# Conditioning by channel-tile pairs of one condition, with the second condition of a batch placed behind the first of the next

## The chip, the cores and the metric

One core of a Trainium2 chip runs one program. The metric is the device time of one execution in microseconds. The engines are TensorE (PE), VectorE (DVE), ScalarE (ACT), GpSimd (POOL) and SyncE (SP, which only issues DMAs); each takes its own instructions in order and waits on semaphores for the others.

## The reference

There are B = 4 batches of T = 512 tokens with C = 512 channels. `x` is conditioned twice, a gated recurrence stands between, and a mixture of experts follows. In short:

```python
def bi_wkv(r, k, w, u, t):            # v = k = fside
    tf = sigmoid(sum(t))
    decay = exp(-exp(w)) * (0.5 + 0.5 * tf)
    ek = exp(min(k, 30)); ekv = ek * k
    # forward and backward scans a = a * decay + ekv, b = b * decay + ek over the 512 tokens
    num = nf + nb - ekv + exp(min(u + k, 30)) * k
    den = df + db - ek  + exp(min(u + k, 30))
    return sigmoid(r) * num / max(den, 1e-8) * (0.8 + 0.2 * tf)

r1 = bi_wkv(x, fside, w1, u1, cond)                       # first condition
z_in, z_dec, z_gate = silu(r1 @ W_in), sigmoid(r1 @ W_decay + bias), sigmoid(r1 @ W_gate)
h = scan(h * z_dec + (1 - z_dec) * z_in)                  # over the tokens
x2 = x + (h * z_gate) @ W_out
r2 = bi_wkv(x2, fside, w2, u2, cond)                      # second condition: same k, other decay and u
out = x2 + moe(r2, Wg, w1, w2)                            # 8 experts, top 2, capacity 640 rows
```

The scans of the second condition do not need `x2`: only its last product, with `sigmoid(x2)`, does.

## The kernel before

`conditioning_and_routing` makes everything up to a table `slots` in DRAM that holds, expert by expert, the rows of `r2`; `experts` then multiplies them by the experts' weights. It starts when the last rows of `slots` are written and read back. All data is kept with channels on partitions, in C / 128 = 4 channel tiles of [128, 512 tokens].

A unit of conditioning is one channel tile of one batch with both conditions; there are 16 units, and unit u uses one of two buffer sets. For a unit:

- ACT copies the transposed `k` out of PSUM (`copy_f`), and makes the exponentials (`exps`); POOL makes the products with `k` (`products`).
- DVE runs `backward`: four scans of 512 tokens (L799, L800). ACT scales the first column of each sum (`first_sums`), and DVE runs `fold`: four more scans (L811), the addition of the own term to both denominators (L816) and two maxima (L818). That sets `s_den`.
- ACT makes the reciprocals as Ln and Exp (`first_reciprocal`), POOL adds the own term of the numerator and multiplies numerator and denominator by the reciprocal (`newton`, six operations), and DVE makes the `ratio` (L829) one unit later.

Engine programs are written as steps, and one step does the conditioning of batch b, the gates of batch b-1 and the tail of batch b-2. The steps are b = 0 to 5, so batch 3 is conditioned in step 3, its gates are made in step 4 and its tail in step 5. On DVE a step ends with `recurrence(b-1)` (scans L847 over the decays), `first_out(b)` (L837, which sets `s_r1` and lets PE start the gates) and `place(b-2)`.

The rest of the path per batch: PE makes 12 gate tiles (`gate`, four matmul instructions each, L437, in three PSUM banks, so that tile k waits until ACT has copied tile k-3 with `gate_sum`); ACT makes Silu and Sigmoid (`inputs`, `gate_functions`); DVE the recurrence; PE `project` (L451); DVE `residual` (L855, gives `x2`); ACT `sigmoid_x2`; DVE `second_out` (L860, gives `r2`); PE `logits` (L481), DVE `select`, PE `places`, DVE `place`, which ends with `dest` (L906); POOL `dispatch`: eight indirect DMAs of 128 rows. Rows of `x2` and `r2` are transposed by PE and copied by ACT (`x2_row`, `r2_row`).

Batch 3's decay and gate tiles are made in another form: ACT and DVE split the operands into a high and a low part (L682, L918), and PE makes three products per tile and channel tile (L431 to L433) instead of one in full precision.

ACT changes its table of functions between {Exp, Ln} and the sets of Sigmoid and Silu; each change is an instruction ACT_TABLE_LOAD.

## Time and profile before

| | us |
|---|---|
| median of 3 runs | 1220.02 (1217.79 to 1220.59) |
| the profiled execution | 1219.18 |
| its span | 1217.1 |
| last conditioning instruction on DVE | 344.7 |
| start of the last batch's recurrence on DVE | 393.4 |
| `dest` of the last batch | 431.3 |
| first large matmul of the experts | 455.5 |

The profile gives each engine's busy time, and the trace gives single instructions with their start and length in microseconds from the start of the span, and in brackets the idle time of the engine before them with what ended it. Several equal instructions in a row stand in one line with a count (x4) and their joint length. PE writes one line entry for each of two passes of a matmul, so one gate tile is "x8". From one line's start to the next is the pitch, which is a little shorter than the length where an engine overlaps instructions. The page of the profile gives for the whole span:

```
PE 1039.4 (85%) x5058; PEld 827.9 (68%) x5059; DVE 677.7 (56%) x970; ACT 533.8 (44%) x914; POOL 322.6 (27%) x251
```

### The profile page before, as it was taken

What the parts mean: (1) busy time and instruction counts of PE and PEld (TensorE: products, weight loads), DVE (VectorE), ACT (ScalarE), POOL (GpSimd) and SP (SyncE); (2) the same over time, 40 slices, a digit from 0 to 9 for tenths busy, and PEclk for the clock granted to TensorE, in tenths of its full rate; (3) what the DMA queues carried; (4) which work ended last, traced back from release to release, by engine and by line L of the source; (5) the groups of instructions that cost most, each with busy time, mean ns of one, the idle gap of its engine ahead of it and who ended that gap; (6) DMA issues with size and microseconds to landing.
All of it is one profiled execution on the core that took longest, in us unless ns stands there. A gap on an engine that the chain in (4) does not pass through costs nothing.

```text
span 1217.1 us, 17595 instructions
## 1 busy us (share of the span) xinstructions
PE 1039.4 (85%) x5058; PEld 827.9 (68%) x5059; DVE 677.7 (56%) x970; ACT 533.8 (44%) x914; POOL 322.6 (27%) x251
## 2 busy tenths in 40 slices
PE   1146797787799829999999999999999999999994
PEld 0022344344348529998999899989898888999883
DVE  6989899899781523334333433355555344343553
ACT  5455746826844212334333433344545334333453
POOL 3878818648630330001100200020201101100302
PEclk9998998997999759999999999999999999999998
DMA  5251340211010452113421621282535234322711
GB/s 191 104 166 35 122 133 35 69 70 69 0 71 35 174 175 104 69 69 118 106 69 69 149 76 69 69 220 91 186 138 186 83 132 134 87 69 69 216 70 21
DMA packets 63406, 125.29 MB, mean 103 GB/s; under 512 B 4726, under 2 KB 4762, under 8 KB 63384
## 3 DMA queue, kind: packets, MB, share of 16 engines
q1 hardware_dynamic: 54728, 107.91, 25.6%
q0 software_dynamic: 8656, 17.13, 7.0%
q8 instruction: 9, 0.15, 0.0%
q14 instruction: 13, 0.11, 0.0%
HBM read 93.04 MB, written 35.22 MB: 105 GB/s over the span
## 4 chain that ended last, share of the span: by engine, by line
PE 58%; issue 1%; ACT 1%; DVEq 1%; DVE 1%; POOL 0%; ACTq 0%; POOLq 0%
PE ps_y L1137 10%; PE ps_y L1138 10%; PE ps_y L1139 10%; PE ps_h L1117 9%; PE ps_h L1119 9%; PE ps_h L1118 9%; PE ps_t L1087 1%; POOL out_dram L1066 0%; ACT xh L1232 0%; ACT y L1239 0%; DVEq L1177 0%; DVE hl L1294 0%; ACT w1h L1204 0%; DVE w1l L1255 0%; ACTq L1177 0%
## 5 line engine op out<-in xcount | busy, mean ns | idle before, releaser
L1117 PE MATMUL ps_h<-xh,w1h 128*128 128x320 f32 (+3 forms) x768 | 247.6, 322 | 7.9 <-issue 4.0
L1119 PE MATMUL ps_h<-xh,w1l 128*128 128x320 f32 (+3 forms) x768 | 243.6, 317 | 0.0
L1118 PE MATMUL ps_h<-xl,w1h 128*128 128x320 f32 (+3 forms) x768 | 243.5, 317 | 0.0
L1066 POOL DMA_INDIRECT out_dram<-y,token x40 | 64.6, 1615 | 657.6 <-ACT y L1239 487.7
L1294 DVE SCALAR_TENSOR_TENSOR hl<-ps_h,hh 128x320 fp32r<-128x320 f32 (+1 forms) x192 | 106.9, 558 | 194.0 <-ACT hh L1228 185.3
L1137 PE MATMUL ps_y<-w2h,hh 128*128 128x512 f32 x528 | 206.5, 391 | 1.9 <-DVE hl L1294 1.9
L1138 PE MATMUL ps_y<-w2h,hl 128*128 128x512 f32 x528 | 206.7, 391 | 0.0
L1139 PE MATMUL ps_y<-w2l,hh 128*128 128x512 f32 x528 | 206.1, 390 | 0.0
L1258 DVE TENSOR_TENSOR w2l<-raw,w2h 128x512 fp32r<-128x512 f32 x128 | 88.6, 692 | 196.5 <-ACT w2h L1207 193.6
L1228 ACT ACTIVATE hh<-ps_h 128x320 fp32r<-128x320 f32 (+1 forms) x192 | 94.4, 492 | 232.4 <-PE ps_h L1119 232.2
L1207 ACT ACTIVATE w2h<-raw 128x512 fp32r x128 | 80.7, 631 | 211.2 <-PE ps_y L1139 210.2
L437 PE MATMUL ps_mm<-ratios,wm 128*128 (+1 forms) x320 | 150.7, 619 | 10.8 <-ACT z_in L607 8.8
L1117 PEld LDWEIGHTS ps_h<-xh,w1h 128*128 128x128 f32 x768 | 145.5, 189 | 16.1 <-issue 8.0
L1118 PEld LDWEIGHTS ps_h<-xl,w1h 128*128 128x128 f32 x768 | 145.5, 190 | 4.9
L1119 PEld LDWEIGHTS ps_h<-xh,w1l 128*128 128x128 f32 x768 | 145.4, 189 | 2.6
L437 PEld LDWEIGHTS ps_mm<-ratios,wm 128*128 128x128 f32 x320 | 61.3, 200 | 79.0 <-issue 67.7
L1139 PEld LDWEIGHTS ps_y<-w2l,hh 128*128 128x128 f32 x528 | 99.1, 188 | 21.3
L1137 PEld LDWEIGHTS ps_y<-w2h,hh 128*128 128x128 f32 x528 | 99.2, 188 | 20.5 <-issue 2.8
L1138 PEld LDWEIGHTS ps_y<-w2h,hl 128*128 128x128 f32 x528 | 99.2, 188 | 17.2
L1255 DVE TENSOR_TENSOR w1l<-raw,w1h 128x512 fp32r<-128x512 f32 x128 | 88.4, 691 | 16.3 <-ACT w1h L1204 12.4
L1204 ACT ACTIVATE w1h<-raw 128x512 fp32r x128 | 79.9, 624 | 0.0
L451 PE MATMUL ps_mm<-z_gate,wm 128*128 128x512 f32 x96 | 49.3, 645 | 20.4 <-DVE z_gate L848 20.4
(194 smaller groups left out, 1290.4 us busy)
## 6 DMA issues: line engine op xcount, KB each, us to landing
raw<-in_L_ffn_w_dram SPq DMA_DIRECT2D x64, 1024.0 KB
slots<-r_rows SPq DMA_DIRECT2D x8, 1302.5 KB, 16.1
rows<-slots SPq DMA_DIRECT2D x8, 1302.5 KB
f_rows<-in_fside_BxSxS_dram SPq DMA_DIRECT2D x5, 1024.0 KB, 5.3
rows<-in_x_dram SPq DMA_DIRECT2D x4, 1024.0 KB, 6.4
out_dram<-x_rows SPq DMA_DIRECT2D x4, 1024.0 KB, 4.9
slots<-r_rows POOLq DMA_DIRECT2D x1, 1302.5 KB
rows<-slots SPq DMA_DIRECT2D x5, 260.5 KB, 4.1
```

Source lines behind the costliest of these rows:

```text
L437: last = nc.tensor.matmul(ps_mm[:, k % 3, :], wm[:, m, dt, e * P:(e + 1) * P], ratios[:, bass.ds(b % 2, 1), 0, dt, :].rearrange("p o t -> ...
L1117: nc.tensor.matmul(o, w1h[:, j, dt, :], xh[:, dt, lo:hi], start=(dt == 0), stop=False)
L1118: nc.tensor.matmul(o, w1h[:, j, dt, :], xl[:, dt, lo:hi], start=False, stop=False)
L1119: last = nc.tensor.matmul(o, w1l[:, j, dt, :], xh[:, dt, lo:hi], start=False, stop=(dt == CT - 1))
L1137: nc.tensor.matmul(ps_y[:, i, :], hh[:, j, tok], w2h[:, j], start=first, stop=False)
L1138: nc.tensor.matmul(ps_y[:, i, :], hl[:, j, tok], w2h[:, j], start=False, stop=False)
L1139: return nc.tensor.matmul(ps_y[:, i, :], hh[:, j, tok], w2l[:, j], start=False, stop=last)
L1207: a.activation(w2h[:, (j + 1) % 2], raw2[:, bass.ds((c + (j + 1) // FC) % 2, 1), (j + 1) % FC] .rearrange("p o n -> p (o n)"), ACT.Copy).t ...
L1228: a.activation(hh[:, j % 2, lo:hi], ps_h[:, bank, 0:hi - lo], ACT.Relu).then_inc(s_hh, 1 if wide else 2)
L1255: v.tensor_tensor(w1l[:, j % 2], raw1[:, bass.ds((c + j // 2) % 2, 1), :, (j + 2) % FC * P:((j + 2) % FC + 1) * P] .rearrange("p o t q -> ...
L1258: v.tensor_tensor(w2l[:, (j + 1) % 2], raw2[:, bass.ds((c + (j + 1) // FC) % 2, 1), (j + 1) % FC] .rearrange("p o n -> p (o n)"), w2h[:, ( ...
L1294: v.scalar_tensor_tensor(out=hl[:, j % 2, lo:hi], in0=ps_h[:, bank, 0:hi - lo], scalar=0.0, in1=hh[:, j % 2, lo:hi].bitcast(F32), op0=ALU.max,
```

## The change

A unit is now two channel tiles of one condition (`UNITS`; c is the condition, b the batch, p the pair). There are 16 units as before, with the same number of scans. The order is c1 of batch 0, c1 of 1, c2 of 0, c1 of 2, c2 of 1, c1 of 3, c2 of 2, c2 of 3. `ek`, `kT` and `ekv` are kept for a whole batch and two batches deep; `euk` also takes the reciprocal, so `own(u + 2)` waits for `newton(u)`. Loops are written out: every engine has a list. All gate tiles have the plain form, and their order is the four inputs, the four decays, the four gates. The recurrence makes its first operation once over [128, 2048]. `x_rows` holds the outgoing rows of `x2` too, and batch 3's rows of `r2` go over the weights `wm`, so that `dispatch(3)` needn't wait for `dispatch(2)`.

```diff
-GATE_TILES = [(0, e) for e in range(CT)] + [(m, e) for e in range(CT) for m in (1, 2)]
+GATE_TILES = [(m, e) for m in range(3) for e in range(CT)]
+UNITS = [(c, b, p) for c, b in ((0, 0), (0, 1), (1, 0), (0, 2), (1, 1), (0, 3), (1, 2), (1, 3)) for p in range(2)]
...
+        def newton(u):
+            r = u % 2
             pool.wait_ge(s_den, u + 1)
             pool.wait_ge(s_eukv, u + 1)
+            for i in range(2):
+                g.tensor_tensor(sums[r][:, i, 0], sums[r][:, i, 0], eukv[:, r, i], ALU.add).then_inc(s_own, 1)
+            pool.wait_ge(s_rec, u + 1)
+            for i in range(2):
+                g.tensor_tensor(sums[r][:, i, 1], sums[r][:, i, 1], euk[:, r, i], ALU.mult)
+            pool.wait_ge(s_own, 2 * u + 2)
+            for i in range(2):
+                last = g.tensor_tensor(sums[r][:, i, 0], sums[r][:, i, 0], euk[:, r, i], ALU.mult)
+            last.then_inc(s_newton, 1)
...
+        newton(14)
+        dispatch(2, 0, TT // 2)
+        newton(15)
+        dispatch(2, TT // 2, TT)
+        dispatch(3, 0, TT)
...
-                pe.wait_ge(s_gl, 3 * CT)
-                high, low = gate_parts[2 * m], gate_parts[2 * m + 1]
...
+        def own(u):
+            c, b, p = UNITS[u]
+            act.wait_ge(s_k, CT * b + 2 * p + 2)
+            if u >= 2:
+                act.wait_ge(s_newton, u - 1)
+            for i in range(2):
+                ct = 2 * p + i
+                a.activation(euk[:, p, i], kT[:, b % 2, ct], ACT.Relu, scale=-1.0,
+                             bias=cap_u[:, c, ct:ct + 1]).then_inc(s_capped, 1)
+            for i in range(2):
+                act.wait_ge(s_capped, 2 * u + i + 1)
+                last = a.activation(euk[:, p, i], euk[:, p, i], ACT.Exp, scale=-1.0, bias=own_bias[:, col(b, c, 2 * p + i)])
+            last.then_inc(s_euk, 1)
+        def first_reciprocal(u):
+            r = u % 2
+            act.wait_ge(s_den, u + 1)
+            act.wait_ge(s_eukv, u + 1)
+            a.activation(euk[:, r], sums[r][:, :, 1], ACT.Ln).then_inc(s_ln, 1)
+            act.wait_ge(s_ln, u + 1)
+            a.activation(euk[:, r], euk[:, r], ACT.Exp, scale=-1.0).then_inc(s_rec, 1)
+        def gate_functions(b):
+            act.wait_ge(s_z, Z_COPIES * b + 2 * CT)
+            a.activation(z_in[:], z_in[:], ACT.Silu)
+            a.activation(z_dec[:], z_dec[:], ACT.Sigmoid).then_inc(s_dec, 1)
...
+        first_reciprocal(2)
+        gate_sum(0, 0)
+        first_sums(3)
+        gate_sum(0, 1)
+        gate_sum(0, 2)
+        own(4)
+        gate_sum(0, 3)
+        gate_sum(0, 4)
+        sigmoid_x(1)
+        exponentials()
+        first_reciprocal(3)
+        gate_sum(0, 5)
+        first_sums(4)
...
+        gate_sum(1, 9)
+        copy_x(2, 2)
+        first_reciprocal(7)
+        first_sums(8)
+        f_tile(3, 0)
+        copy_x(2, 3)
+        gate_functions(1)
...
         def recurrence(b):
+            steps = Steps(dve, s_rec_steps, REC_STEPS * b)
+            dve.wait_ge(s_dec, b + 1)
+            steps.do(v.scalar_tensor_tensor(out=z_in[:], in0=z_dec[:], scalar=1.0, in1=z_in[:],
+                                            op0=ALU.subtract, op1=ALU.mult))
             for e in range(CT):
+                steps.mark(v.tensor_tensor_scan(z_in[:, e], z_dec[:, e], z_in[:, e], 0.0, ALU.mult, ALU.subtract))
+            for e in range(CT):
+                dve.wait_ge(s_rec_steps, REC_STEPS * b + 2 + e)
                 dve.wait_ge(s_gates, CT * b + e + 1)
                 v.tensor_tensor(z_gate[:, e], z_gate[:, e], z_in[:, e], ALU.mult).then_inc(s_y, 1)
```

DVE's list, with what was in the steps now between the units (`cond` is `backward`, `fold` and the `ratio` of the unit before):

```
cond 0..2, first_out(0); cond 3; backward 4, fold 4, ratio 3, first_out(1), recurrence(0)
backward 5, fold 5, residual(0), ratio 4; cond 6, second_out(0); backward 7, select(0), fold 7, ratio 6, place(0)
backward 8, recurrence(1), fold 8, ratio 7, first_out(2); backward 9, residual(1), fold 9, ratio 8; cond 10, second_out(1)
backward 11, select(1), fold 11, ratio 10, place(1), recurrence(2); cond 12, first_out(3), residual(2); cond 13
cond 14, second_out(2); backward 15, recurrence(3), fold 15, select(2), ratio 14, place(2)
residual(3), ratio 15, second_out(3), select(3), place(3)
```

PE's list: transposes of batches 0 and 1; `gate(0, 0..11)`, `project(0)`; then per batch b = 1, 2, 3 `gate(b, k)` with the rows, logits and places of batch b-1 and the transposes of later batches between, and `project(b)`; at the end the rows, logits and places of batch 3.

## Rows read from the trace of the kernel before

**Rows 1.** Windows: busy time of each engine, PE clock, DMA share and rate

```profile
344.00:407.00 63.00, 61.72 (x247) 39.51 (x246) 29.89 (x76) 29.19 (x44) 9.95 (x8) 0.97 0.23 84
407.00:432.00 25.00, 17.14 (x87) 13.99 (x85) 10.11 (x39) 9.54 (x14) 9.38 (x8) 0.62 0.34 128
sum 432.00, PE 296.35 PEld 163.58 DVE 344.06 ACT 239.21 POOL 241.74; mean PE 42.34 PEld 23.37 DVE 49.15 ACT 34.17 POOL 34.53
```

**Rows 2.** Timeline of DVE: start, length, engine, line, what, idle before

```profile
344.05 0.69 DVE L829 SCALAR_TENSOR_TENSOR ratios<-sums_odd 128x512 f32 x1
...
393.38 0.69 DVE L845 SCALAR_TENSOR_TENSOR z_in<-z_dec,z_in 128x512 f32<-128x512 f32 x1 [16.34 <-ACT z_gate L618]
...
431.16 0.17 DVE L906 CAST dest<-dest_f 128x8 uint32<-128x8 f32 x1
```

**Rows 3.** Timeline of DVE: the start, then units 4 and 5

```profile
15.88 1.22 DVE L799 TENSOR_TENSOR_SCAN sums_even<-ps_decay,k_and_exp_k 128x512 f32<-128x512 f32 x1 [1.62 <-POOL ekv L341]
...
84.28 1.21 DVE L799 TENSOR_TENSOR_SCAN sums_even<-ps_decay,k_and_exp_k 128x512 f32<-128x512 f32 x1
...
88.76 4.77 DVE L811 TENSOR_TENSOR_SCAN sums_even<-ps_decay,sums_even 128x511 f32<-128x511 f32 x4
93.45 1.28 DVE L816 TENSOR_TENSOR sums_even<-sums_even,euk 128x1024 f32<-128x1024 f32 x1
94.77 0.88 DVE L818 TENSOR_SCALAR sums_even<-sums_even,den_min 128x512 f32<-128x512 f32 x2
...
105.11 2.06 DVE L816 TENSOR_TENSOR sums_odd<-sums_odd,euk 128x1024 f32<-128x1024 f32 x1
107.20 2.78 DVE L818 TENSOR_SCALAR sums_odd<-sums_odd,den_min 128x512 f32<-128x512 f32 x2
109.90 2.29 DVE L829 SCALAR_TENSOR_TENSOR ratios<-sums_even 128x1024 f32<-128x1024 f32 x1
```

**Rows 4.** Timeline of PE: gates of batch 0, a projection, a gate and a transpose

```profile
82.57 12.02 PE L437 MATMUL ps_mm<-ratios,wm 128*128 128x512 f32 x24 [0.26 <-DVE ratios L837]
...
153.10 2.07 PE L451 MATMUL ps_mm<-z_gate,wm 128*128 128x512 f32 x2 [6.59 <-DVE z_gate L848]
...
168.96 0.60 PE L402 MATMUL ps_f<-ident,f_rows 128*128 128x128 f32 x4
169.40 3.60 PE L437 MATMUL ps_mm<-ratios,wm 128*128 x8
172.83 0.60 PE L463 MATMUL ps_to<-ident,z_dec 128*128 128x128 f32 x4
```

**Rows 5.** Timeline of ACT: a copy, two Ln, a table load, a Silu

```profile
66.87 0.60 ACT L560 ACTIVATE xT<-ps_x 128x512 f32<-128x512 f32 x1 [1.27 <-PE ps_x L413]
...
97.97 1.17 ACT L589 ACTIVATE recip<-sums_even 128x512 f32<-128x512 f32 x2
...
142.64 1.28 ACT L611 ACT_TABLE_LOAD   x1
143.94 1.91 ACT L611 ACTIVATE z_in<-z_in 128x2048 f32<-128x2048 f32 x1
```

**Rows 6.** Timeline of POOL: a product, an indirect DMA of the dispatch

```profile
119.15 1.27 POOL L356 TENSOR_TENSOR sums_odd<-sums_odd,recip 128x512 f32<-128x512 f32 x1
...
256.95 0.99 POOL L374 DMA_INDIRECT slots<-r_rows,dest  x1 [0.30 <-issue]
```

**Rows 7.** Timelines of DVE, PE and POOL: the tail of batch 3

```profile
412.88 2.35 DVE L860 SCALAR_TENSOR_TENSOR sig<-ratios,neg_scale,sig 128x2048 f32<-128x2048 f32 x1 [1.98 <-ACT sig L637]
...
416.57 6.84 PE L481 MATMUL ps_small<-wg,sig 128*128 128x8 f32 x32
...
432.20 1.16 POOL L374 DMA_INDIRECT slots<-r_rows,dest  x1 [13.54 <-DVE dest L906]
```

**Rows 8.** Groups by line (busy, mean ns) and a DVE timeline row: the split form

```profile
L433 PE MATMUL ps_mm<-r_high,w_gate_low 128*128 128x512 f32 x16 | 6.2, 391 | 0.0
...
353.22 2.49 DVE L918 TENSOR_TENSOR w_decay_low<-wm,w_decay_high 128x512 fp32r<-128x512 f32 x4
```

More of the change, by code:

```diff
@@ L736, in _ @@
         act.preload_act_table_set("natural_log_exp_and_others")
-        copy_f(0, 0)
+        f_tile(0, 0)
+        f_tile(0, 1)
+        ek_exp(0, 0)
         act.wait_ge(s_setup_v, SETUP_MD2)
@@ new lines, in _ @@
+        f_tile(1, 0)
+        f_tile(1, 1)
+        ek_exp(1, 0)
+        own(2)
+        sigmoid_x(0)
+        exponentials()
+        first_reciprocal(1)
+        for ct in range(CT):
+            copy_x(1, ct)
+        first_sums(2)
+        f_tile(1, 2)
+        f_tile(1, 3)
+        ek_exp(1, 1)
+        own(3)
+        first_reciprocal(2)
[6 more added lines that the diff above has]
+        gate_sum(0, 4)
@@ new lines, in _ @@
+        gate_sum(1, 7)
+        copy_x(2, 0)
+        gate_sum(1, 8)
+        copy_x(2, 1)
+        gate_sum(1, 9)
[5 more added lines that the diff above has]
+        gate_functions(1)
+        sigmoid_x(2)
+        exponentials()
+        own(9)
+        first_reciprocal(8)
+        first_sums(9)
+        f_tile(3, 1)
+        ek_exp(3, 0)
+        sigmoid_x2(1)
+        exponentials()
+        own(10)
+        gate_sum(2, 0)
@@ new lines, in _ @@
+        r2_row(1, 2)
+        r2_row(1, 3)
+        own(12)
+        gate_sum(2, 9)
+        copy_x(3, 0)
+        copy_x(3, 1)
+        copy_x(3, 2)
+        copy_x(3, 3)
+        probabilities(1)
+        gate_functions(2)
+        sigmoid_x(3)
+        exponentials()
+        first_reciprocal(11)
+        first_sums(12)
+        own(13)
+        first_reciprocal(12)
+        sigmoid_x2(2)
+        exponentials()
+        first_sums(13)
+        gate_sum(3, 0)
+        x2_row(2, 0)
+        x2_row(2, 1)
@@ new lines, in _ @@
+        gate_sum(3, 1)
+        x2_row(2, 2)
+        x2_row(2, 3)
+        own(14)
+        gate_sum(3, 2)
+        gate_sum(3, 3)
+        first_reciprocal(13)
+        gate_sum(3, 4)
+        first_sums(14)
+        gate_sum(3, 5)
+        gate_sum(3, 6)
+        own(15)
+        gate_sum(3, 7)
+        gate_sum(3, 8)
+        gate_sum(3, 9)
+        first_reciprocal(14)
+        first_sums(15)
+        gate_functions(3)
+        exponentials()
+        for i in range(TT):
+            r2_row(2, i)
@@ new lines, in _ @@
+        ratio(2)
+        backward(4)
+        fold(4)
+        ratio(3)
+        first_out(1)
+        recurrence(0)
+        backward(5)
+        fold(5)
+        residual(0)
+        ratio(4)
+        backward(6)
+        fold(6)
+        ratio(5)
+        second_out(0)
+        backward(7)
+        select(0, routing[0])
+        fold(7)
+        ratio(6)
+        place(0, routing[0])
+        backward(8)
+        recurrence(1)
+        fold(8)
+        ratio(7)
+        first_out(2)
+        backward(9)
@@ new lines, in _ @@
+        residual(1)
+        fold(9)
+        ratio(8)
+        backward(10)
+        fold(10)
+        ratio(9)
+        second_out(1)
+        backward(11)
+        select(1, routing[1])
+        fold(11)
+        ratio(10)
+        place(1, routing[1])
+        recurrence(2)
+        backward(12)
+        fold(12)
+        ratio(11)
+        first_out(3)
+        residual(2)
+        backward(13)
+        fold(13)
+        ratio(12)
+        backward(14)
+        fold(14)
+        ratio(13)
@@ L951, in _ @@
+        second_out(2)
+        backward(15)
+        recurrence(3)
+        fold(15)
+        select(2, routing[2])
+        ratio(14)
+        place(2, routing[2])
+        residual(3)
+        ratio(15)
+        second_out(3)
+        select(3, routing[3])
+        place(3, routing[3])
         dve.wait_ge(s_count, 1)
```

753 lines of the change are left out of this document (377 added, 376 removed).

## The prediction

> **What bounds the kernel now.** I read the windows first, then the timelines of DVE, PE, ACT and POOL through the first 432 us. The experts' part is bound by PE and isn't edited, so only the moment at which the last batch's rows are placed can move. DVE carries 344 of the first 432 us [rows 1], and until 344.7 it is what is late: it goes from unit to unit with little idle time. From there on DVE works 40 of 88 us [rows 1]. That stretch is a chain for batch 3 alone: its gates need its `first_out`, then come functions, the recurrence at 393.4, projection, `r2`, logits, and `dest` at 431.3 [rows 2]. So the 344 us are DVE's and the 87 us behind them are latency. The reader should see in [rows 2] the 16 us in which DVE waits for the gates.
>
> **What one unit costs.** Backward is 4.5 us (84.28 to 88.76), fold 4.7, the addition 1.3, the maxima 0.8 (two, pitch) [rows 3]. Where POOL works at the same time the addition takes 2.06, the maxima 2.78, the ratio 2.29 instead of 1.2 [rows 3]. So a unit costs 12.5 to 16.3. The new unit has the same instructions on DVE; the work of POOL is nine products a unit on average, at 1.22 us pitch [rows 6], as before. Newton now adds both own terms while ACT makes Ln and Exp (2.1 us at 1024 columns, as in [rows 5]), so it takes 7.4 us behind `s_den`. I take 13 to 15.5 a unit, and nothing saved here.
>
> **What it removes.** The operand splits go: 7.5 us of DVE (three rows of 2.49, of which one stands in [rows 8]) and 6.5 of ACT. Plain tiles cost PE 3.44 us (169.40 to 172.83) [rows 4] against about 2.8 for twelve products of 0.23 us pitch with start; eight tiles are 5 us more of PE [rows 8]. Both hang on the same chain, and with batch 3's gates now beside conditioning neither is late by itself: nearest to nothing.
>
> **What it moves.** `first_out(3)` comes after unit 11, so four units stand beside the gates of batch 3. The gain is what the chain behind 344.7 loses. But every engine's list is in order, and I walked the four lists against each other. The walk shows that DVE will wait for ACT and PE in places where it didn't before. Its steps:
>
> *Start.* ACT makes two tiles of `k` before the first exponential and POOL two products before `s_ekv`: backward(0) at 18.2 instead of 15.9 [rows 3].
>
> *To first_out(0).* Units 0 and 1 are 12 and 13.3 us. In ACT `copy_x(1, 0..3)` stands ahead of `first_sums(2)`, each waiting for a transpose, 1.85 us a round (1.27 + 0.60) [rows 5]; fold(2) waits 5.3 us. s_r1 at 68.3.
>
> *Recurrence 0.* Gate tiles end 12.0 us after r1 for the first three, then every 3.44 [rows 4]. `gate_sum(0, 4)` (r1 + 19.5) and `sigmoid_x` with two table loads (1.28 + 1.91 + 1.28 = 4.5) [rows 5] stand ahead of `first_reciprocal(3)` and `first_sums(4)`. These come at r1 + 27 where DVE is ready at r1 + 18: it waits 9. Ten gate tiles end at r1 + 36.1, then a sum 0.6, `f_tile` 1.2, and Silu and Sigmoid with their loads 6.4 [rows 5]: s_dec at 113.0, DVE waits 6.
>
> *The ring of one batch.* From the recurrence's start the first y is 7.5 us off (2.3 + 4.6 + 0.6, scans as in [rows 3]), the projection 15.9 (153.10 to 168.96) [rows 4], then PE's list, then 6.4 of functions. Batch 1: eleven gates 37.9, fifteen groups of transposes at 0.44 [rows 4], logits 3.6 (an estimate: about half of the 6.84 that they take at the low granted clock [rows 1, 7]), places 0.3, a copy 0.6: 79 us, recurrence(1) at 192.2 where DVE is ready at 179.6 (12.6 idle). Batch 2: twelve gates, fourteen groups, logits, plus 2.3 for backward(9) ahead of residual(1), 5 for rows and `f` tiles that ACT holds behind `own(10)` and `first_reciprocal(9)`, 1 for copies: 90 us, recurrence(2) at 282.1; DVE idles 5 at select(1), 6 at place(1) and 4 here. Batch 3: `first_out(3)` and residual(2) hold gate(3, 0) until 307.6; ten gates and four groups end at 343.8, then sum, reciprocal(14), first_sums(15): recurrence(3) at 353.3, 7 us after backward(15).
>
> *The tail.* Recurrence 9.3, fold, addition, maxima: 369.4. select(2) about 3; place(2) waits for the projection (360.8 + 14.7) and places: dest(2) at 377.8. POOL: `dispatch(2, 0, 2)` stands ahead of `newton(15)`: four DMAs at 1.29 (0.99 + 0.30) [rows 6], then six products 7.4: 390.6. This is a new wait, 13 us, and ratio(15) and all of batch 3's routing are behind it. ratio 1.2, second_out 2.35: 394.2. From the end of second_out to the end of dest the old tail takes 16.1 us (415.23 to 431.33) [rows 2, 7]; 1.3 of it was rows of x2 ahead of the logits, which are done by then: 14.4 with the other order of places. dest(3) ends at 408.6.
>
> The old one ended at 431.3. The sum is 22.7 us less: 1219.2 (the profiled execution, span 1217.1) gives 1196.5; the median is 0.8 above that execution, so 1197.3.
>
> **Unknown costs and their bounds.** An `own` has 4 ACT instructions of 0.6 [rows 5], 2.5 us, but waits for newton two units back; where it blocks is in the walk, and the bound is 0 to 9.9 (7.4 + 2.5) a batch; I am near 2, as newton is mostly done. POOL's collisions with DVE: 12.5 to 16.3 a unit; in the walk DVE has some 70 us of slack by waiting, so most of this is hidden; bound 0 to 12 for the last units. Load of the first expert chunk and stores now lie under conditioning, and the DMA share is 0.23 in the stretch where they lay before [rows 1]; nothing, up to 2 us. The experts' rows are read and written as before; PE's clock at the start of the experts after a short busy tail is as before (0.62 in the tail [rows 1]).
>
> **A page of the Trainium skill against this.** A table load takes 1.28 us here, and the next function starts 1.30 after it [rows 5]. ACT's new list puts about twelve of them on the chain of recurrences. The Trainium skill, page "ScalarE: Activation LUTs", section "What ACT_TABLE_LOAD costs", says that each switch also has a drain of about 1380 ns, 2.66 us in all. By that rule as a mechanism of this kernel the chain would be longer by twelve further waits. I price it by rows: twelve loads of 1.28 once more [rows 5] are 15.4, and the time 1212.7.
>
> **The rivals.**
> 1. DVE stays the bound: the waits in the walk don't come about, since ACT and PE are early. For it: DVE was the bound for 344 us [rows 1]. Then DVE's 344 less 7.5 and less 4 of setup run from 18.2, with 7 of them in the tail: ratio(15) near 344, dest(3) near 361, 70 us less: 1149. Against it: ten gates at 3.44 and a projection of 15.9 alone are more than three units of DVE.
> 2. Slower: ACT's in-order list. Each `own(u)` waits for a newton that waits for a reciprocal that stands in the same list, and behind it stand the sums that free PE's three banks. If each batch pays 9.9 us more, the four rings pay 39.6: 1219.2 - 22.7 + 39.6 + 0.8 = 1237. It decides from 5.7 a ring. For it: the idle time that the walk already finds in front of each recurrence; against it: newton is done 5 us before most owns.
> 3. The end doesn't move, because newton(15) behind the dispatch, or DMAs of four batches drained together, take all: 1220. The old dispatch(3) started 0.9 us after dest [rows 2, 7], so nothing of that kind is seen.
> 4. The second load price above: 1213.
>
> **How the numbers follow.** The walk 0.70, rival 1 0.08, rival 2 0.12, rival 3 0.04, rival 4 0.06. Forecast 1197. The walk by itself has 1186 to 1209 (eight of its waits each off by 1 to 2 us, and POOL's bound). With the neighbours the range for 8 in 10 is 1180 to 1216. About 0.2% is what a measurement of this kernel tells from no change: faster 0.84 (walk, 1 and 4), same 0.04, slower 0.12.
>
> **What would show it.** recurrence starts near 113, 192, 282 and 353, each after idle time of DVE that ACT ends; first scan at 18.2; POOL's newton(15) after four indirect DMAs; dest of batch 3 near 409; the experts' part equal in length. If DVE is dense and the recurrences come every 60 us, rival 1 is right; if the gates' PSUM banks wait for ACT through most of a batch, rival 2; if the gap between a table load and its function is over a microsecond, rival 4. The prediction is wrong if an ordering wait that I read as already met is late in each batch.

## The result and the profile after

The changed kernel takes 1210.01 us (median of four, 1209.27 to 1212.65) against 1219.48 (1217.79 to 1220.59): a ratio of 0.993 with a 95% interval of 0.9918 to 0.9941. It is 9.5 us faster where 22.7 were forecast. The profiled execution took 1209.29, its span is 1207.6 (1217.1 before). From the last `dest` to the end the two are alike: 785.6 us (1207.6 less 421.97) and 785.8 (1217.1 less 431.33). All that changed lies ahead of that `dest`.

First the conditioning, cut at the four recurrences. Columns: busy time (and count) of PE, PE's weight loads, DVE, ACT and POOL, then PE's granted clock, the DMA share and GB/s.

```profile
core 0: us, PE busy (x) PEld busy (x) DVE busy (x) ACT busy (x) POOL busy (x), PEclk, DMA share, GB/s
16.00:114.28 98.28, 57.43 (x156) 29.34 (x156) 75.77 (x65) 62.65 (x88) 67.51 (x47) 1.00 0.62 197
114.28:198.88 84.60, 71.04 (x238) 36.58 (x238) 73.21 (x86) 51.66 (x74) 45.75 (x32) 0.92 0.10 38
198.88:293.72 94.84, 72.46 (x230) 36.69 (x230) 80.96 (x92) 52.23 (x73) 56.04 (x40) 0.86 0.13 45
293.72:365.68 71.96, 61.90 (x172) 29.64 (x172) 64.76 (x55) 42.55 (x56) 50.65 (x36) 0.92 0.21 74
365.68:422.00 56.32, 35.20 (x146) 24.18 (x145) 32.00 (x87) 18.78 (x27) 17.36 (x14) 0.66 0.15 57
```

No engine is full in any stretch: DVE works 81 of 95 us in the third row, PE 72. DVE had worked 344 of 432 us [rows 1]; over these five rows it works 327 of 406. So something other than one engine's work sets each length. DVE's timeline shows what it stands still for (start, length, line, operation, and in brackets the idle time ahead with what ended it):

```profile
114.28 2.29 DVE L1005 SCALAR_TENSOR_TENSOR z_in<-z_dec,z_in 128x2048 f32<-128x2048 f32 x1 [5.98 <-ACT z_dec L661]
121.09 6.71 DVE L1012 TENSOR_TENSOR z_gate<-z_gate,z_in 128x512 f32<-128x512 f32 x4
...
198.88 2.29 DVE L1005 SCALAR_TENSOR_TENSOR z_in<-z_dec,z_in 128x2048 f32<-128x2048 f32 x1 [10.08 <-ACT z_dec L661]
...
205.69 4.61 DVE L1012 TENSOR_TENSOR z_gate<-z_gate,z_in 128x512 f32<-128x512 f32 x4
...
245.75 8.97 DVE L979 TENSOR_TENSOR sums_even<-sums_even,euk 128x1024 f32<-128x1024 f32 x1
...
287.29 0.19 DVE L1056 TENSOR_REDUCE prob_sum<-prob 128x4 f32<-128x32 f32 x1 [8.66 <-ACT prob L706]
...
293.72 2.29 DVE L1005 SCALAR_TENSOR_TENSOR z_in<-z_dec,z_in 128x2048 f32<-128x2048 f32 x1 [3.95 <-ACT z_dec L661]
...
300.53 2.47 DVE L1012 TENSOR_TENSOR z_gate<-z_gate,z_in 128x512 f32<-128x512 f32 x4
...
365.68 2.29 DVE L1005 SCALAR_TENSOR_TENSOR z_in<-z_dec,z_in 128x2048 f32<-128x2048 f32 x1 [6.80 <-ACT z_dec L661]
...
404.29 1.23 DVE L993 SCALAR_TENSOR_TENSOR ratios<-sums_odd 128x1024 f32<-128x1024 f32 x1 [10.44 <-POOL sums_odd L346]
...
421.80 0.17 DVE L1068 CAST dest<-dest_f 128x8 uint32<-128x8 f32 x1
```

These answer [rows 2] and [rows 7]: the last recurrence starts at 365.68 instead of 393.38, the last `dest` at 421.80 instead of 431.16. 27.7 us were won on the way to the last recurrence, and 18.3 of them were given back behind it: 56.3 us from recurrence(3) to the end of `dest`(3) where the old tail had 38.0. In front of every recurrence DVE waits for ACT's decays. The 18.3 us have two parts. From the start of the recurrence to `residual` are 25.5 us where the old kernel had 14.2: the first y comes 7.5 us behind the start instead of 2.7, as the recurrence now makes each kind of operation for all channel tiles before the next kind; the projection takes 15.7 instead of 14.0; and `residual`(3) starts 2.2 us behind its end, where the old one started 2.5 ahead of it, since place(2) stands in front and waits 3.5 us for PE's places. From `residual` to `second_out` are 14.5 where it had 5.3, as ratio(15) stands still for 10.44. The rest is 2.1 us shorter.

POOL's timeline shows the second part, as the walk had it: four indirect DMAs and six products stand between `dest`(2), at 391.23, and ratio(15).

```profile
392.03 1.00 POOL L356 DMA_INDIRECT slots<-r_rows,dest  x1 [28.26 <-DVE dest L1068]
...
395.91 0.98 POOL L356 DMA_INDIRECT slots<-r_rows,dest  x1 [0.30 <-issue]
396.90 2.50 POOL L340 TENSOR_TENSOR sums_odd<-sums_odd,eukv 128x512 f32<-128x512 f32 x2
...
401.79 2.47 POOL L346 TENSOR_TENSOR sums_odd<-sums_odd,euk 128x512 f32<-128x512 f32 x2
```

Beside the walk (a ring is the stretch from one recurrence's start to the next):

| | walk | measured | longer by |
|---|---|---|---|
| recurrence(0) starts | 113.0 | 114.28 | 1.3 |
| to recurrence(1) | 79.2 | 84.60 | 5.4 |
| to recurrence(2) | 89.9 | 94.84 | 4.9 |
| to recurrence(3) | 71.2 | 71.96 | 0.8 |
| to the end of `dest`(3) | 55.3 | 56.29 | 1.0 |
| end of `dest`(3) | 408.6 | 421.97 | 13.4 |

So the chain is the one I walked, and two of its rings carry 10.3 of the 13.4 us. PE's timeline shows where. The lines are the first projection matmuls, the first gate tiles behind `residual`, the logits, and the gate tiles behind those; a gate tile alone takes 3.60.

```profile
122.84 2.08 PE L443 MATMUL ps_mm<-z_gate,wm 128*128 128x512 f32 x2 [9.08 <-DVE z_gate L1012]
...
140.43 3.67 PE L426 MATMUL ps_mm<-ratios,wm 128*128 128x512 f32 x8 [1.29 <-DVE xT L1017]
...
161.38 3.74 PE L474 MATMUL ps_small<-wg,sig 128*128 128x8 f32 x32
...
166.67 4.49 PE L426 MATMUL ps_mm<-ratios,wm 128*128 128x512 f32 x8
...
226.72 5.25 PE L426 MATMUL ps_mm<-ratios,wm 128*128 128x512 f32 x8 [4.83 <-DVE xT L1017]
...
240.29 1.11 PE L402 MATMUL ps_f<-ident,f_rows 128*128 128x128 f32 x4 [2.44 <-ACT kT L607]
...
267.37 5.29 PE L426 MATMUL ps_mm<-ratios,wm 128*128 128x512 f32 x8
```

Ring 1, from 114.28 to 198.88, has these excesses. The first y comes 8.56 after the recurrence's start, not 7.5 (the four products beside POOL take 6.71). The projection takes 16.3 instead of 15.9 (to 139.14). PE then stands still for 1.29, as `residual(0)` stands in DVE's list behind fold(5). From the first gate at 140.43 to the functions' table load at 192.43 are 52.0 us where I had 49.0 (11 gates 37.9, 15 groups 6.6, logits 3.6, places and a copy 0.9); of these 3.0, some 1.7 lie between the logits' start and the end of the gate tile behind them (9.6 us against 3.6 + 0.9 + 3.4). The sum is 1.06 + 0.4 + 1.29 + 3.0 = 5.75, against 5.4 (the walk's own terms add up to 78.8, not to its 79.2). Ring 2: y 0; projection -0.4 (15.5); PE stands still for 4.83 where I had 2.3; and from gate(2, 0) at 226.72 to the table load at 287.27 are 60.6 where I had 57.9. That is 4.8 against 4.9, and the last piece holds two gate tiles at a lower clock, 1.65 and 1.7 longer than 3.60.

### The profile page after: what moved, and what is told of

Read it like the earlier page. It is cut to its first block, busy times and chain, and to the rows that moved or that the text cites. A ratio compares the mean times of both kernels' runs of the same rounds, so it can differ in the third digit from the quotient of the medians.

```text
span 1207.6 us, 16920 instructions
## 1 busy us (share of the span) xinstructions
PE 1044.7 (87%) x5022; PEld 823.6 (68%) x5023; DVE 664.6 (55%) x942; ACT 530.4 (44%) x848; POOL 320.0 (26%) x248
## 3 DMA queue, kind: packets, MB, share of 16 engines
q1 hardware_dynamic: 54200, 106.86, 25.3%
## 4 chain that ended last, share of the span: by engine, by line
PE 59%; issue 1%; ACT 1%; DVEq 1%; DVE 1%; POOL 0%; ACTq 0%; POOLq 0%
PE ps_y L1350 10%; PE ps_y L1351 10%; PE ps_y L1352 10%; PE ps_h L1330 10%; PE ps_h L1332 9%; PE ps_h L1331 9%; PE ps_t L1300 1%; POOL out_dram L1279 0%; ACT xh L1445 0%; ACT y L1452 0%; DVEq L1390 0%; DVE hl L1507 0%; ACT w1h L1417 0%; DVE w1l L1468 0%; ACTq L1390 0%
## 5 line engine op out<-in xcount | busy, mean ns | idle before, releaser
L426 PE MATMUL ps_mm<-ratios,wm 128*128 128x512 f32 x384 | 175.3, 612 | 20.6 <-DVE ratios L999 12.0
L426 PEld LDWEIGHTS ps_mm<-ratios,wm 128*128 128x128 f32 x384 | 74.1, 198 | 109.3 <-issue 106.0
## 6 DMA issues: line engine op xcount, KB each, us to landing
slots<-r_rows SPq DMA_DIRECT2D x8, 1302.5 KB, 15.5
```

What stands on the lines that cost most here:

```text
L426: last = nc.tensor.matmul(ps_mm[:, k % 3, :], wm[:, m, dt, e * P:(e + 1) * P], ratio_of(0, b)[:, dt], start=(dt == 0), stop=(dt == CT - 1))
```

## The experiments

All times are medians, against 1210.0 for the changed kernel; single executions of one kernel differ by 3 to 9 us and the ratios are known to some 0.2 to 0.4%, so I read medians for whether a change counts at all and the profiled execution for where, and say so where the two disagree. The changed kernel was not run again beside the later ones; the kernel before was, and its medians lay between 1217.97 and 1219.91. So 1 to 2 us between two medians are not told from nothing.

Part of the spread shows in the traces: the four products of a recurrence take 2.47, 4.61 or 6.71 us, by how POOL's products fall beside them, and for recurrence(1) that changes between traces of programs that are the same up to there. In the changed kernel's trace they take 4.61 in recurrence(1) and 2.47 in recurrence(2). With newton(15) ahead of the dispatch, an edit that acts 180 us later, recurrence(1) has 2.47, PE waits 1.91 instead of 4.83 ahead of gate(2, 0), and ring 2 is 91.9 instead of 94.8. DVE's timeline of it:

```profile
206.32 2.47 DVE L1011 TENSOR_TENSOR z_gate<-z_gate,z_in 128x512 f32<-128x512 f32 x4
```

Recurrence(2) is as unsteady: in three traces whose edits don't touch it (`sigmoid_x(1)` late, logits twice, no maxima) its products take 4.61, and ring 3 is 75.5, 75.3 and 74.6 instead of 72.0. A ring read from one trace can be 3 us off by that alone.

**Is DVE's work the bound, before and after?** In the changed kernel the maxima of units 3 to 14 were left out, and in the kernel before all of them:

```diff
+            if 3 <= u <= 14:
+                dve.sem_inc(s_den, 1)
+                return
             for i in range(2):
                 last = v.tensor_scalar(sums[p][:, i, 1], ..., ALU.max)
```

> The changed kernel without the maxima of the denominators with 1e-8 in units 3 to 14: 24 DVE instructions, some 17 us of DVE busy time, are left out. Theory R: most of it goes into waiting before the recurrences; only what stands between a recurrence and the residual, or between a residual and first_out, counts: 1203 to 1209. Rival D: 1192 to 1196.

> The kernel before the change, without the maxima that keep the denominators from zero (left out of all 16 pairs; the denominators are not bounded then). They are 32.7 us of DVE in 432. In the changed kernel the same cut of units 3 to 14 (24 maxima, some 17 us with their collisions) moved the time by 0.1. If it is true that DVE's work was the bound before and isn't any more (theory W), the kernel before gains most of the 31 us that lie ahead of its 344th us, less what GpSimd and ScalarE then hold up: 1190 to 1200 against 1219.5. If DVE was not the bound before either (my reading of it was wrong from the start), it gains 0 to 6: 1213 to 1219.

Measured: 1210.14 (ratio to before 0.9925, 0.9907 to 0.9944) after the change, 0.1 from nothing; 1201.31 (0.9856, 0.9835 to 0.9878) before it, 18.6 less than the 1219.91 beside it. In the latter the last recurrence moved from 393.38 to 376.45:

```profile
376.45 0.69 DVE L843 SCALAR_TENSOR_TENSOR z_in<-z_dec,z_in 128x512 f32<-128x512 f32 x1 [16.33 <-ACT z_gate L618]
```

The two cuts are not of one size: 32.7 us of DVE before the change, 14.8 us after it (the changed kernel's maxima of these units; the expectation said 17). Still, 18.6 us for the one stand against nothing for the other, where I had expected 1203 to 1209. DVE's occupancy was the bound and isn't any more. Ring 1 kept its length (84.67 instead of 84.60, with 3.1 us less DVE work in it); ring 2 was 2.3 shorter and ring 3 2.6 longer, so that the three together were 251.8 instead of 251.4. That rules out rival 1, and with it every account of the missing 13 us by the sum of DVE's work; where single instructions of DVE stand in the chain is another matter.

**The tail.** newton(15) ahead of the whole dispatch of batch 2:

```diff
-        dispatch(2, 0, TT // 2)
         newton(15)
-        dispatch(2, TT // 2, TT)
+        dispatch(2, 0, TT)
```

> The changed kernel with newton(15) ahead of all of dispatch(2) on POOL. Theory R (the path that sets the end is a ring through ACT, PE and DVE, and in the tail ratio(15) waits for newton(15), which stands behind four DMAs that wait for dest(2)): ratio(15) starts near 395 instead of 404.3, second_out near 396 to 398, dest(3) 8 to 10 us earlier, the whole 1200 to 1202. Rival D (DVE's own work or the drain of the DMAs sets the end): no change, 1210.

Measured: 1203.82 (0.9882, 0.9865 to 0.9898), 6.2 less. DVE's timeline:

```profile
392.40 1.21 DVE L992 SCALAR_TENSOR_TENSOR ratios<-sums_odd 128x1024 f32<-128x1024 f32 x1
394.46 2.35 DVE L1022 SCALAR_TENSOR_TENSOR sig<-ratios,neg_scale,sig 128x2048 f32<-128x2048 f32 x1 [0.85 <-ACT sig L684]
```

ratio(15) no longer waits, and recurrence(3) to `dest`(3) falls from 56.3 to 48.5, 7.8 less. So this wait was real, and it is the reordering's own: a dispatch put ahead of a product that a longer chain waits for. The walk called it 13 us; DVE stood still for 10.44, and 7.8 came back, as `second_out` then waits for `residual`(3) and ACT's sigmoid. The other part of the longer tail, from the recurrence to `residual`(3), was left as it is in every run: what its three pieces are worth is read from the traces and not tested.

**`residual(1)` ahead of backward(9).** In the changed kernel PE stands still for 4.83 us ahead of gate(2, 0).

```diff
-        backward(9)
         residual(1)
+        backward(9)
```

> The changed kernel with residual(1) ahead of backward(9) on DVE. Theory R: gate(2, 0) waits only for residual(1), which DVE begins 4 us after the projection ends because of the four scans in front; the third recurrence (293.7) comes 3.5 to 4.5 us earlier, the fourth and dest(3) 2 to 4.5, the whole 1206 to 1208. Rival D: DVE does the same work in another order, 1210 plus or minus 0.5.

Measured: 1215.57 (0.9968, 0.9951 to 0.9984), 5.6 slower, against my expectation. PE's timeline of it:

```profile
223.22 3.60 PE L426 MATMUL ps_mm<-ratios,wm 128*128 128x512 f32 x8
...
230.10 0.66 PE L402 MATMUL ps_f<-ident,f_rows 128*128 128x128 f32 x4 [2.40 <-ACT kT L607]
...
239.43 1.11 PE L456 MATMUL ps_to<-ident,xT 128*128 128x128 f32 x4 [5.24 <-ACT rows L695]
```

The wait for `residual` is gone and gate(2, 0) is 3.5 us earlier, but DVE stood still for 2.24 us in front of `residual(1)`, and backward(9) came 2.7 us later (224.09 for 221.38). ACT's list has `first_sums(9)` ahead of `f_tile(3, 1)`, of the sigmoid of x2 and of the copies that PE needs: ACT waited 9.26 us for DVE there (4.51 in the changed kernel), and PE in turn 2.40 and 5.24 us for ACT. Ring 2 grew from 94.8 to 97.8 (198.80 to 296.62), as the profiled execution grew by 2.8 (1212.08 for 1209.29), about half of what the medians say. The rest fits the products: in this trace those of recurrence(1) took 2.47, as with newton(15) first, and against ring 2 there (91.9) this one is 5.9 longer, with backward(9) 5.6 later behind the recurrence's start.

**`sigmoid_x(1)` and its table loads behind `first_sums(4)`.**

```diff
         gate_sum(0, 4)
-        sigmoid_x(1)
-        exponentials()
         first_reciprocal(3)
         gate_sum(0, 5)
         first_sums(4)
+        sigmoid_x(1)
+        exponentials()
```

> The changed kernel with sigmoid_x(1) and its two table loads moved behind first_sums(4) on ACT, so that DVE's 8.4 us of waiting at fold(4) goes. Theory R: the wait lies beside the 36 us of PE's gates of batch 0, so the first recurrence starts at 114.3 as before or within 1 us of it, and the whole is 1210 plus or minus 1; the idle time appears in front of the recurrence instead. Rival D (each wait of DVE that the change brought is lost time): 1202 to 1204.

Measured: 1210.08 (0.992, 0.9904 to 0.9937), no change, as expected. DVE's wait for `first_sums(4)` fell from 8.42 to 4.60, and the one for the decays ahead of recurrence(0) rose from 5.98 to 9.73. Freeing DVE ahead of this recurrence bought nothing, as that waits for PE's gates and ACT's functions.

**The clock ahead of the projection.** Extra matmuls fill the 9 to 14 us in which PE has nothing to do between the last gate and the first y (shown for batch 0; batches 1 and 2 have 14 and 20):

```diff
+        keep_clock(0, 12)      # 12 matmuls of 384 columns into ps_to
         project(0)
```

> The changed kernel with 12, 14 and 20 extra matmuls of 384 columns (their result isn't used; identity times the projection's weights, into a bank that is free) ahead of the projections of batches 0, 1 and 2, where TensorE has nothing to do for 9 to 14 us. Nothing else is changed. Theory C (part of the 4 to 5 us by which a ring is longer than I worked out is TensorE at its lower clock after idle time: in the changed kernel the first projection tiles of 2.08 for two matmuls against 0.43 a matmul later, and the first gate after the logits 4.49 and 5.29 against 3.60): the projections of batches 0 to 2 take 14.0 instead of 15.3 to 16.3, and the three rings get 1.3 to 2.3 shorter each: 1204 to 1206 against 1210.0. The gates behind the logits (4.49, 5.29) do not get shorter. Theory W (the rings hang on TensorE's list, but the clock costs nothing beyond what the first matmuls show): 1208 to 1210. Theory D (DVE's own work sets the rings): 1210.

Measured: 1212.07 (0.9939, 0.9919 to 0.9959): not faster. The projections did get faster, 14.0 each instead of 16.3, 15.5 and 15.8, and DVE's order took it back. PE's timeline:

```profile
124.13 1.12 PE L443 MATMUL ps_mm<-z_gate,wm 128*128 128x512 f32 x2 [1.34 <-DVE z_gate L1020]
...
141.73 6.32 PE L426 MATMUL ps_mm<-ratios,wm 128*128 128x512 f32 x8 [3.60 <-DVE xT L1025]
...
229.47 5.12 PE L426 MATMUL ps_mm<-ratios,wm 128*128 128x512 f32 x8 [6.31 <-DVE xT L1025]
```

PE is done sooner and waits longer for `residual`, 3.60 and 6.31 instead of 1.29 and 4.83. The gate tile behind the first of them runs slower, 6.32 instead of 3.67. `residual(0)` starts 25.3 us behind the recurrence's start in both traces, whenever PE is done. Ring 1 became 86.1 long. So the low clock at the projection is hidden by what DVE has in front of `residual`; theory C is wrong for it.

**GpSimd kept off the recurrence.** newton(4)'s multiplications and products(9) wait for the y:

```diff
             pool.wait_ge(s_rec, u + 1)
+            if u == 4:
+                pool.wait_ge(s_y, CT)
...
+            if u == 9:
+                pool.wait_ge(s_y, 2 * CT)
```

> The changed kernel, where two pieces of GpSimd's work wait until DVE has made the y of a recurrence: the multiplications of newton(4) (they run during recurrence(0)) and products(9) (during recurrence(1)). Theory P (DVE's two-operand instructions are held up by GpSimd's, and that is on the ring: the four products behind the scans took 6.71 us in recurrence(0), 4.61 in recurrence(1), 2.47 in the other two): both take 2.5, the first y comes about 1 us earlier and the last 4 and 2 us, so residual(0) and residual(1) come 1 to 2 us earlier each: 1206 to 1208 against 1210.0, if the later newton(4) isn't itself waited for. Theory W (what counts is the first y, since the projection takes the y in turn and is longer than the products): 1209 to 1211. If GpSimd's delay is passed on to the next ratio: up to 1213.

Measured: 1206.62 (0.9898, 0.9875 to 0.9921), 3.4 less. In recurrence(0) the four products take 2.47 instead of 6.71:

```profile
122.84 2.47 DVE L1016 TENSOR_TENSOR z_gate<-z_gate,z_in 128x512 f32<-128x512 f32 x4
```

What counted was the last y and all of DVE's work behind it, not the first: `residual(0)` is 21.3 us behind the recurrence's start instead of 25.3, and in ring 1 PE goes from projection to gates without a pause. Ring 1 is 81.8 (84.6), ring 2 92.2 (94.8). Ring 3 is 75.5 (72.0): GpSimd works beside recurrence(2), where the products took 4.61 instead of 2.47, and gate(3, 0) waited 4.34 instead of 2.53 and ran in 5.37 instead of 3.67. As that happens in traces without this edit too, it isn't shown that the edit brought it; it does show in the length of ring 3 what a collision in this place costs.

**The logits.** Twice as many of batches 0 and 1:

```diff
-        logits(0)
+        logits(0, 2)
```

> The changed kernel, with the logits of batches 0 and 1 made twice (32 matmuls of 8 columns more, the same result). Theory W (TensorE's list sets the rings, so each us of TensorE between a batch's first_out and the next recurrence is a us of time): rings 1 and 2 are 3.5 us longer each, the third is not: 1217 against 1210.0. Theory C (small matmuls lower the clock for what follows): the gate behind the logits takes 5.3 to 7.0 instead of 4.49 and 5.29, 1 to 2 us a ring more: 1219 to 1221. Theory D (DVE's work sets the rings, it idles 8 to 10 us ahead of each recurrence, but for other reasons): 1210 to 1212.

Measured: 1223.46 (1.0034, 1.0017 to 1.0051), 13.5 slower, more than any theory had. PE's timeline:

```profile
162.69 9.53 PE L474 MATMUL ps_small<-wg,sig 128*128 128x8 f32 x64
...
173.81 5.53 PE L426 MATMUL ps_mm<-ratios,wm 128*128 128x512 f32 x8
...
271.26 8.73 PE L474 MATMUL ps_small<-wg,sig 128*128 128x8 f32 x64
```

The second set took 5.8 and 5.1 us where the first takes 3.7 and 3.6: the clock falls while PE makes matmuls of 8 columns. Ring 1 grew by 6.9 and ring 2 by 5.3. This profiled execution was the longest of the seven, at 1227.15. Its ring 3 (75.3) is 3.3 longer too, and its products of recurrence(2) took 4.61, as in the other traces with a ring 3 of 75; the tail is 1.3 longer, and that stays open.

**The logits of batch 1 behind the last gate tile** (select(1) and place(1) then stand behind recurrence(2), ACT's exponential of the probabilities behind the functions, and `sigmoid_x(3)` waits for these logits):

```diff
-        logits(1)
...
         transpose_x(3, 3)
+        logits(1)
         places(1)
```

> The changed kernel, with the logits of batch 1 behind the last gate tile and the transposes of x3 on TensorE (select(1) and place(1) then follow recurrence(2) on DVE, and the exponential of the probabilities follows the functions on ScalarE). In the changed kernel the logits take 3.5 us in the middle of batch 2's gates, and the gate tile behind them 5.29 instead of 3.60. If both are terms of the ring (3.5, which I had in my sum, and 1.7, which I hadn't), the ring of batch 2 falls from 94.8 to 89 or 90, and to 85 if the 8.66 and 3.95 us that DVE stands still ahead of recurrence(2) were the exponential's doing alone. The time is 1203 to 1206 against 1210.0 then. If the lower clock comes from something else than the small matmuls, only 3.5 is gained: 1206 to 1207. If routing later holds up GpSimd's dispatch and newton(12) behind it: 1208 to 1213.

Measured: 1208.37 (0.9917, 0.9892 to 0.9942), 1.6 less, which isn't told from nothing, and not the 1203 to 1206 that I expected. PE's timeline, the gate tile that stood behind the logits, and DVE's, the recurrence:

```profile
264.67 3.60 PE L426 MATMUL ps_mm<-ratios,wm 128*128 128x512 f32 x8
```

```profile
289.81 2.29 DVE L1007 SCALAR_TENSOR_TENSOR z_in<-z_dec,z_in 128x2048 f32<-128x2048 f32 x1 [12.71 <-ACT z_dec L661]
```

The gate tile takes 3.60 instead of 5.29, and ring 2 is 90.2 instead of 94.8. That settles the 1.7 us: it is the logits' doing. Ring 3 is 76.6 instead of 72.0: select and place of batch 1 now stand between recurrence(2) and `residual(2)` on DVE, and the 4.6 us are back. Also, DVE's 8.66 and 3.95 are one wait, 12.71 when the exponential is out of the way; what it waits for is the decays.

**The plain gates alone**, in the kernel before: batch 3's gates as the others, and no splitting of operands.

```diff
-            if isinstance(b, int) and b == B - 1 and k >= CT:
-                ...three products for each channel tile...
...
-                    if gates and not cond:
-                        gate_operands()
```

> The kernel before the change, with batch 3's gates in plain form like the others and without the splitting of the weights and ratios (7.5 us of DVE, three of 2.49, and 6.5 us of ScalarE) that they need. TensorE gets 8 tiles of 3.44 for tiles of about 2.8, 5 us more, on the chain of batch 3 that ends the conditioning; DVE gets 7.5 us less ahead of that chain, while it is the bound. My reading in the prediction was 'nearest to nothing': 1216 to 1221 against 1219.5. If the operands' work lay beside other work, 1223 to 1225. If DVE's time is all that counts, 1212.

Measured: 1223.22 (1.003, 1.002 to 1.0041), 3.7 slower. The last recurrence starts at 398.31 instead of 393.38. PE's 5 us more are all on the chain, and the operands' 7.5 us of DVE were worth little: `second_out(2)` came only 1.4 us later than before, with 9.56 us of idle time in front of it instead of 2.34.

**The functions early.** If PE's list and the functions set the rings, the functions needn't wait for the last gate tiles, since the recurrence needs only z_in and the decays (tiles 0 to 7; shown for batch 1, the others are alike):

```diff
         gate_sum(1, 7)
+        decay_functions(1)     # Silu of z_in, Sigmoid of z_dec, s_dec
...
         gate_functions(1)      # now the sigmoids of z_gate alone
```

> The changed kernel, in which ScalarE makes Silu of z_in and Sigmoid of z_dec (all that a recurrence needs to start) right behind the sum of gate tile 7 of each batch, not behind that of tile 9 and the copies of the next batch's x; the sigmoids of z_gate stay where they were. Theory W (the recurrence waits for TensorE's list and for the functions, so the four last gate tiles can lie beside functions and scans): the idle time of DVE ahead of the recurrences, 5.98, 10.08, 3.95 and 6.80 in the changed kernel, goes for the most part; 1186 to 1198 against 1210.0. Theory O (it is the order of lists: ScalarE stands still in front of the functions for gate 7 and keeps back sums, logarithms and own terms, which DVE needs, and loads two more tables in each batch): the recurrences come earlier but folds and ratios behind them later; 1203 to 1214. Theory D (DVE's work sets the rings): 1210.

Measured: 1200.24 (0.9844, 0.9817 to 0.987), 9.8 less, between what the two theories had. DVE's timeline:

```profile
182.38 2.26 DVE L1011 SCALAR_TENSOR_TENSOR z_in<-z_dec,z_in 128x2048 f32<-128x2048 f32 x1
...
196.99 3.41 DVE L1018 TENSOR_TENSOR z_gate<-z_gate,z_in 128x512 f32<-128x512 f32 x4 [7.74 <-ACT z_gate L668]
```

recurrence(1) starts as soon as DVE comes to it, 16.5 us earlier than in the changed kernel, and then DVE waits 7.74 us inside it for the sigmoids of z_gate. So ring 1 is 13.4 us shorter (71.2) and ring 3 2.3 (69.6), but ring 2 is 5.1 longer (100.0, with 11.64 us of waiting for the exponential ahead of place(1), which stood in front of recurrence(2)) and the tail 4.3. The tail's part is a collision: beside POOL's products the scans of recurrence(3) took 5.60 instead of 4.57 and its products 5.64 instead of 2.47, 4.2 us together. Both theories have a part: the functions' wait was real, and the order of lists took back nearly half.

**Several moves together**: newton(15) first, the functions early, the exponential and the places of batch 1 earlier, recurrence(2) ahead of place(1).

> The changed kernel with several moves at once: newton(15) ahead of the dispatch of batch 2 (which gave 6.2 us by itself), the functions of z_in and z_dec behind gate tile 7, the exponential of batch 1's probabilities ahead of the copies of x3 on ScalarE, batch 1's places ahead of the transposes of x3 on TensorE, and recurrence(2) ahead of place(1) on DVE (there DVE idles 8.66 us for the exponential, then 3.95 for the decays). Theory W: the ring of batch 2 loses up to 12 us, that of batch 1 up to 10, the tail 8 to 10: 1172 to 1190. Theory O: 1190 to 1203, newton(15)'s gain and little more.

Measured: 1187.15 (0.9713, 0.9678 to 0.9749). `dest`(3) ends at 403.05. This version beats both kernels, by 32.4 and 22.9 us.

The same with newton(4) and products(9) behind the y:

> The version with several moves (1187.2), with the multiplications of newton(4) and products(9) on GpSimd held back until recurrence(0) and recurrence(1) have made their y. In the changed kernel that gave 3.4 us, of which the trace shows 2.8 in the ring of batch 1 and 2.6 in that of batch 2, and 3.5 given back in that of batch 3. With the functions early, DVE is dense around the recurrences and the projection waits for the gates' sigmoids rather than for the first product, so I expect less: 1184 to 1188. If the collisions are on the path here too: 1180 to 1184.

Measured: 1184.6 (0.9709, 0.9677 to 0.9741). `dest`(3) ends at 401.35, 1.7 earlier; the executions of both versions lie between 1181.4 and 1190.4, so it isn't told apart from the one without it.

## Why the prediction went wrong

*What bounds the kernel* was right: DVE's occupancy up to its 344th us, and from there batch 3's chain. Taking out maxima showed both halves, 18.6 us before and nothing after.

*What it removes.* "Neither is late by itself: nearest to nothing" was wrong as a statement on the kernel before: the plain gates alone cost 3.7 us, as they are on the chain that ended there. For the sum it made no difference, since the walk of batch 3 took every tile at 3.44.

*Start, to first_out(0), recurrence 0* were right to about a microsecond: backward(0) at 18.17 (forecast 18.2), fold(2) waits 4.69 (5.3), fold(4) 8.42 (9), DVE 5.98 ahead of recurrence(0) (6), at 114.28 (113.0).

*The ring of one batch* is the step that failed, by 10.3 of the 13.4 us: 79.2 and 89.9 us were forecast for the first two rings, and they measured 84.6 and 94.8. Its mechanism was right, PE's list plus functions, and these of its terms were too small:

- "The first y is 7.5 us off": the term should have been the last y and DVE's list behind it. The products beside POOL took 6.71 and 4.61 us, not 2.5, and pushed `residual` behind the end of the projection. Keeping POOL away gave 2.8 and 2.6 us in the two rings, and the second ring was 2.9 shorter where POOL's products happened to miss the recurrence. I had written of POOL's collisions that "most of this is hidden", with a bound of 12 for the last units only; I had not looked at where a collision stands ahead of something PE waits for.
- "2.3 for backward(9) ahead of residual(1)": it was 4.8, and the gate tile behind that pause took 5.25, not 3.60. Where the collision was missing it was 1.9, and the tile took 3.67, so this excess is the one above once more.
- "Logits 3.6": their own length was right, but the gate tile behind them is 0.9 and 1.7 us longer. Moving batch 1's away shortened its ring by 4.6, my own term and this one nearly. I could have seen it: in the kernel before, products behind the logits at 370.91 already take 0.63 where the ones before take 0.39.

```profile
370.00 0.39 PE L433 MATMUL ps_mm<-r_high,w_gate_low 128*128 128x512 f32 x1
...
370.91 3.63 PE L481 MATMUL ps_small<-wg,sig 128*128 128x8 f32 x32
...
376.33 0.63 PE L433 MATMUL ps_mm<-r_high,w_decay_low 128*128 128x512 f32 x1
```

Collisions and clock hang together: PE pauses for `residual`, and the clock of the tile behind can be lower. Counted with what they bring, the collisions are 2.8 of the 5.4 us in ring 1 and 2.6 to 2.9 of the 4.9 in ring 2, and the logits' 1.7 in each are most of the rest. Some 1.2 us over the two rings stay open. The clock at the projection is none of it.

*The tail* was right: newton(15) behind four DMAs was forecast at 390.6 to end and ended 404.26, 13.7 later with everything ahead of it 12.4 later (365.68 for 353.3), and undoing the order gave 6.2 us. Only its price as "a new wait, 13 us" was high: DVE stood still for 10.44, and 7.8 came back in the trace.

*The rivals.* Rival 1 (DVE stays the bound) is ruled out. Rival 2 (ACT's order holds the banks) isn't what happened in the gates: PE has its tiles at 3.60 without a pause, but for 2.44 us at 240.29 in ring 2. Its idea, that a wait in ACT's in-order list comes back elsewhere, is what made the earlier `residual(1)` 5.6 us slower. Rival 3 was closer than its chance of 0.04 said, as 18.3 of the 27.7 us were given back in the tail, but not all, and less than half of it by the dispatch that it named. Rival 4, the table load at twice its price, fell on one row. By the Trainium skill, page "ScalarE: Activation LUTs", section "What ACT_TABLE_LOAD costs", some 1.38 us of drain belong to each switch; here the function starts 1.29 after its load and no more. ACT's timeline:

```profile
287.27 1.28 ACT L660 ACT_TABLE_LOAD   x1
288.56 1.91 ACT L660 ACTIVATE z_in<-z_in 128x2048 f32<-128x2048 f32 x1
```

*The range* of 1180 to 1216 held the time near its upper end; the walk's own, 1186 to 1209, did not. All errors had one sign: the walk had no term for a wait that I hadn't found, and "eight waits each off by 1 to 2 us" was taken as if they could cancel. Here they did not.

## What to carry to other kernels

When work is put beside other work, the bound can change from an engine's busy time to a chain through several in-order lists. From then on removing that engine's work can be worth nothing (maxima: 18.6 us before, nothing after), and an earlier step is worth only what the next wait leaves of it: four of my edits moved a wait by 3 to 5 us and won 2 at most, or lost. Look for a wait that stands for more than its consumer needs (functions behind tiles that the recurrence doesn't use: 9.8 us; a product behind DMAs: 6.2 us), and move those together (22.9 us). When walking such a chain, price each matmul row by what PE does ahead of it, look at which of DVE's products POOL can fall beside, and give the range more room on the slow side.

## What the hardware showed that I had not expected

An addition of two SBUF tiles on DVE that takes 1.20 us took 8.97, as long as POOL's products followed each other without a gap. POOL's timeline of the changed kernel, beside the row at 245.75 above:

```profile
243.81 2.51 POOL L340 TENSOR_TENSOR sums_odd<-sums_odd,eukv 128x512 f32<-128x512 f32 x2
246.26 2.50 POOL L343 TENSOR_TENSOR sums_odd<-sums_odd,euk 128x512 f32<-128x512 f32 x2
248.71 2.48 POOL L346 TENSOR_TENSOR sums_odd<-sums_odd,euk 128x512 f32<-128x512 f32 x2
251.15 1.26 POOL L328 TENSOR_TENSOR ekv<-ek,kT 128x512 f32<-128x512 f32 x1
252.38 1.26 POOL L329 TENSOR_TENSOR ekv<-ek,kT 128x512 f32<-128x512 f32 x1
253.91 1.93 POOL L332 TENSOR_TENSOR eukv<-euk,kT 128x512 f32<-128x512 f32 x1 [0.28 <-ACT euk L625]
```

POOL's first gap is at 253.64, and the addition ended at 254.72, 1.1 us later, about its own length. The Trainium skill, page "SBUF — State Buffer", section "Summary: rules for kernel authors", says that where the DVE instruction has two SBUF inputs and the GpSimd one reads SBUF, the second to issue blocks fully until the first finishes; here it was held through seven instructions, not one. The scans with their decays in PSUM kept 1.19 to 1.22 in all 64 rows of this trace. The recurrence's scans, which read two SBUF tiles, take 4.57 for the four; in the version with several moves those of recurrence(2) took 7.66, and there POOL's products start inside them.

TensorE's granted clock fell in a stretch of small matmuls, with PE busy throughout. The windows of the kernel with the logits twice, ahead of the logits, in them and behind them (the last number but two is the granted clock, 1.00 for 2.4 GHz and 0.50 for 1.2 GHz, in between a mean of the two):

```profile
152.30:162.60 10.30, 10.30 (x26) 4.34 (x24) 10.15 (x8) 9.01 (x13) 6.17 (x4) 1.00 0.59 210
164.00:172.00 8.00, 8.00 (x54) 8.00 (x54) 3.12 (x3) 0.60 (x2) 7.12 (x6) 0.72 0.15 55
172.00:179.00 7.00, 7.00 (x18) 4.03 (x18) 6.53 (x23) 1.20 (x2) 0.00 (x0) 0.59 0.00 0
```

32 matmuls of 8 columns took 3.7 us and the next 32 took 5.8, and the gate tile behind them 5.53 instead of 3.60. It was lower as well where PE had stood still, but not in step with the pause: the gate tile behind 1.29 us took 3.67, behind 2.53 us 3.67, behind 3.60 us 6.32, behind 4.83 us 5.25 (granted clock 0.50 at its start).
